# Tokens and hidden rows split into fp16 parts first and turned by transposing DMAs, in a cross-attention block with an MLP

## What is computed

```
q  = LN(x) @ Wq.T + bq ;  k, v = LN(ctx) @ Wk.T + bk, LN(ctx) @ Wv.T + bv
s  = q k.T / sqrt(32) - scale[h] * |xy_q - xy_k| + offset[h] ;  masked keys: -inf
x1 = x + softmax(s) v @ Wo.T + bo
out = x1 + gelu(LN(x1) @ W1.T + b1) @ W2.T + b2        (W1: 2048 x 512)
```

## Time and profile before

| | us |
|---|---|
| median of 3 runs | 1339.89 (1337.30 to 1341.35) |
| profiled execution | 1340.12 |
| its span, first to last instruction | 1338.3 |
| TensorE busy | 1265.7 |
| VectorE, ScalarE, GpSimd busy | 888.0, 831.9, 752.0 |
| share of the sixteen DMA engines, hardware queue | 67.7% |

### The profile page before, as it was taken

How to read it: one execution, slowest core, us unless ns; L and a number is a source line. 1 busy time by engine, 2 the same in 40 slices (tenths; PEclk the granted TensorE clock), 3 DMA queues, 4 the chain that set the end, 5 groups by cost and what they waited for, 6 DMA issues and landing times.

```text
span 1338.3 us, 29112 instructions
## 1 busy us (share of the span) xinstructions
PE 1265.7 (95%) x10624; PEld 881.7 (66%) x10624; DVE 888.0 (66%) x2299; ACT 831.9 (62%) x1905; POOL 752.0 (56%) x871
## 2 busy tenths in 40 slices
PE   5777668999999999999999999999999999999998
PEld 5556336666767676766667676767677676766664
DVE  6577777857667586867677675868676775656311
ACT  4566667766666666666666666666667676664231
POOL 2244556765756576665647565766656575647310
PEclk9775789999999999999999999999999999999999
DMA  6336769676867776775858676777868686657334
GB/s 232 101 76 157 194 166 216 139 186 143 201 150 185 148 179 157 177 173 150 189 146 202 142 174 162 171 173 161 181 146 194 147 188 135 164 144 182 89 109 142
DMA packets 366830, 216.58 MB, mean 162 GB/s; under 512 B 282192, under 2 KB 307040, under 8 KB 366688
## 3 DMA queue, kind: packets, MB, share of 16 engines
q1 hardware_dynamic: 366688, 214.73, 67.7%
HBM read 109.66 MB, written 12.58 MB: 91 GB/s over the span
## 4 chain that ended last, share of the span: by engine, by line
PE 85%; DMA 4%; ACT 4%; DVE 3%; SPq 2%; issue 1%; POOL 0%; DVEq 0%; ACTq 0%
PE ps_down L585 24%; PE ps_up L571 24%; PE ps_qk L500 11%; PE ps_vo L523 6%; PE ps_vo L526 6%; PE ps_s L537 4%; PE ps_pv L552 4%; DMA c_stage<-in_w 3%; PE ps_pv L558 2%; PE ps_pv L479 2%; ACT square_half L648 1%; SPq L333 1%; PE ps_vo L486 1%; SPq L342 1%; PE ps_up L450 1%
## 5 line engine op out<-in xcount | busy, mean ns | idle before, releaser
L984 DVE CUSTOM_DVE_ANT_0 soft<-ps_s,soft,factor 128x256 f32<-128x256 f32 x512 | 226.6, 480 | 266.5 <-PE ps_s L537 265.4
L571 PE MATMUL ps_up<-hT,w 128*128 128x256 f16 x3072 | 378.5, 273 | 0.0
L585 PE MATMUL ps_down<-w,hid 128*128 128x512 f16 x1536 | 372.6, 379 | 0.6 <-DMA w<-x_scratch 0.3
L571 PEld LDWEIGHTS ps_up<-hT,w 128*128 128x128 f16 x3072 | 301.1, 98 | 87.8
L1156 POOL TENSOR_SCALAR p_nat<-soft 128x512 f16<-128x512 f32 x256 | 182.4, 712 | 268.4 <-ACT soft L704 250.7
L704 ACT ACTIVATE soft<-soft,neg_max 128x256 f32<-128x256 f32 x512 | 255.3, 501 | 106.1 <-DVE neg_max L984 100.7
L736 ACT ACTIVATE u<-ps_up,bias,up_scale 128x256 f32<-128x256 f32 x256 | 143.4, 560 | 172.7 <-PE ps_up L571 171.4
L1163 POOL TENSOR_SCALAR soft<-dist,scale_neg,offset 128x512 f32<-128x512 f32 x256 | 237.9, 929 | 3.3 <-DVE p_nat L995 3.3
L585 PEld LDWEIGHTS ps_down<-w,hid 128*128 128x128 f16 x1536 | 148.3, 97 | 133.7 <-DMA w<-x_scratch 2.4
L995 DVE SCALAR_TENSOR_TENSOR p_nat<-soft,p_nat 128x512 f16<-128x512 f32 x256 | 200.2, 782 | 0.5 <-POOL p_nat L1156 0.5
L697 ACT ACTIVATE qk_parts<-ps_qk,bias_qkv 128x512 f16<-128x512 f32 x128 | 87.7, 685 | 86.8 <-DMA stack<-stack 43.4
(11 more groups left out here) (119 smaller groups left out, 1586.7 us busy)
## 6 DMA issues: line engine op xcount, KB each, us to landing
w<-x_scratch SPq DMA_DIRECT2D x256, 256.0 KB, 2.8
stack<-qk_parts SPq DMA_DIRECT2D x256, 96.0 KB
raw<-in_ctx SPq DMA_DIRECT2D x32, 256.0 KB, 3.4
raw<-in_x SPq DMA_DIRECT2D x32, 256.0 KB, 3.3
c_stage<-in_w SPq DMA_DIRECT2D x8, 1024.0 KB, 6.6
x<-in_x SPq DMA_DIRECT2D x32, 256.0 KB, 4.2
out<-x SPq DMA_DIRECT2D x32, 256.0 KB, 3.3
tok_rows<-in_tok_xy SPq DMA_DIRECT2D x16, 256.0 KB, 4.0
```

The costliest lines, as they stand in the source:

```text
L571: mm = e.matmul(ps_up[s % 2][:, 0:L], w_1_sb[:, wp, k, m * P:(m + 1) * P], hT[:, b % 2, xp, k, :], start=(k, wp, xp) == (0, 0, 0), stop=(k ...
L585: mm = e.matmul(ps_down[tt][:], hid[:, chunk % HID_RING, i, hp, tt * P:(tt + 1) * P], w_2_sb[:, s % W2_RING, wp, :], start=(m == 0 and (hp ...
L984: e.tensor_tensor_reduce(soft[:, ring, lc, :], ps_s[:, lc * T:(lc + 1) * T], soft[:, ring, lc, :], factor[:, 0:1], 3.0e38, ALU.add, ALU.mi ...
```

## The change

x_nat and h_nat are new: a normalised tile, still by token, as two fp16 parts side by side, 128 x 1024, one buffer each. ScalarE writes the high part (`x_hi`, `h_hi`) and VectorE the low part (`x_lo`, `h_lo`) from SBUF; SyncE turns both by one transposing DMA (`x_turn`, `h_turn`), of the shape of p_turn's, into xT and hT, whose layout becomes [buffer, which, token tile, part and k, 128]. The fp32 transposes on TensorE are gone, and with them the users of ps_pv and ps_vo beside attention and projections. Slots of batch 0: norm_apply -24 + 4n as before, x_hi and x_lo -23 + 4n, x_turn -22 + 4n; h_apply 26 and 28 (later in VectorE's order within the slot), h_hi and h_lo 27 and 29, h_turn 28 and 30. The parts of a tile wait until the tile before has been turned. To make room, soft has 4 entries for 5 and pT 5 for 6, and bias_tile(i) moves from slot i - 2 to slot i - 1.

```diff
-        SOFT_RING, NAT_RING, PT_RING, STACK_RING, DIST_RING, X1_RING, U_RING, HID_RING, W2_RING = 5, 4, 6, 2, 2, 6, 3, 2, 3
+        SOFT_RING, NAT_RING, PT_RING, STACK_RING, DIST_RING, X1_RING, U_RING, HID_RING, W2_RING = 4, 4, 5, 2, 2, 6, 3, 2, 3
...
-        xT = sb("xT", [P, 2, 2, 2, KT, L], F16)
+        x_nat = sb("x_nat", [P, 2, D], F16)
+        xT = sb("xT", [P, 2, 2, 2, 2 * KT, P], F16)
...
-        hT = sb("hT", [P, 2, 2, KT, L], F16)
+        h_nat = sb("h_nat", [P, 2, D], F16)
+        hT = sb("hT", [P, 2, 2, 2 * KT, P], F16)
...
-        X_TURN, V_PROJ, O_PROJ, H_TURN = -23, (1, 4), (24, 26), (28, 30)
+        X_APPLY, V_PROJ, O_PROJ, H_APPLY = -24, (1, 4), (24, 26), (26, 28)
...
             def load_tile(b, n):
-                gate.wait_ge(s_xtr, n_tile(b - 1, n))
+                gate.wait_ge(s_xlo, n_tile(b - 1, n))
...
+            def x_turn(b, n):
+                gate.wait_ge(s_xlo, n_tile(b, n))
+                gate.wait_ge(s_qk, n_qk(4 * (b - 2) + 3, n // 2))
+                gate.wait_ge(s_v, n_half(b - 2, 1))
+                e.dma_start_transpose(xT[:, b % 2, n // 2, n % 2, :, :], x_nat[:].rearrange("p w d -> p (w d)")).then_inc(s_xt, DMA)
+
+            def h_turn(b, tt):
+                gate.wait_ge(s_hlo, n_half(b, tt))
+                gate.wait_ge(s_m1, MT * (b - 1))
+                e.dma_start_transpose(hT[:, b % 2, tt, :, :], h_nat[:].rearrange("p w d -> p (w d)")).then_inc(s_ht, DMA)
...
                     p_turn(i)
+                for n in range(4):
+                    for b in due(slot, X_APPLY + 2 + 4 * n, BATCH, B):
+                        x_turn(b, n)
+                for tt in range(LC):
+                    for b in due(slot, H_APPLY[tt] + 2, BATCH, B):
+                        h_turn(b, tt)
...
-            def x_turn(b, n):
-                gate.wait_ge(s_ap, n_tile(b, n))
-                gate.wait_ge(s_id, ID_IDENT)
-                gate.wait_ge(s_xlo, n_tile(b, n) - 1)
-                gate.wait_ge(s_y, 4 * (b - 2) + n + 1)
-                for k in range(KT):
-                    tr = e.transpose(ps_pv[:, k * P:(k + 1) * P], raw[:, n, k * P:(k + 1) * P], ident[:])
-                tr.then_inc(s_xtr)
-
-            def h_turn(b, tt):
-                gate.wait_ge(s_hap, n_half(b, tt))
-                gate.wait_ge(*vo_empty(("h", b, tt)))
-                for k in range(KT):
-                    tr = e.transpose(ps_vo[:, k * P:(k + 1) * P], x1_n[:, k * P:(k + 1) * P], ident[:])
-                tr.then_inc(s_htr)
...
-                        gate.wait_ge(s_xlo, n_tile(b, 2 * which + 1))
+                        gate.wait_ge(s_xt, DMA * n_tile(b, 2 * which + 1))
...
-                                              xT[:, b % 2, which, xp, k, :], start=(k, wp, xp) == (0, 0, 0), stop=last)
+                                              xT[:, b % 2, which, :, xp * KT + k, :], start=(k, wp, xp) == (0, 0, 0), stop=last)
...
-                gate.wait_ge(s_xlo, min(G + 8, 4 * B))
...
-                gate.wait_ge(s_hlo, n_half(b, 1))
+                gate.wait_ge(s_ht, DMA * n_half(b, 1))
...
             def x_hi(b, n):
-                gate.wait_ge(s_xtr, n_tile(b, n))
-                gate.wait_ge(s_qk, n_qk(4 * (b - 2) + 3, n // 2))
-                gate.wait_ge(s_v, n_half(b - 2, 1))
-                e.activation(xT_parts(b, n)[HI], turned(ps_pv), ACT.Copy).then_inc(s_xhi)
+                gate.wait_ge(s_ap, n_tile(b, n))
+                gate.wait_ge(s_xt, DMA * (n_tile(b, n) - 1))
+                e.activation(x_nat[:, HI, :], raw[:, n, :], ACT.Copy).then_inc(s_xhi)
 
             def h_hi(b, tt):
-                gate.wait_ge(s_htr, n_half(b, tt))
-                gate.wait_ge(s_m1, MT * (b - 1))
-                e.activation(hT_parts(b, tt)[HI], turned(ps_vo), ACT.Copy).then_inc(s_hhi)
+                gate.wait_ge(s_hap, n_half(b, tt))
+                gate.wait_ge(s_ht, DMA * (n_half(b, tt) - 1))
+                e.activation(h_nat[:, HI, :], x1_n[:], ACT.Copy).then_inc(s_hhi)
...
-                    for b in due(slot, X_TURN + 1 + 4 * n, BATCH, B):
+                    for b in due(slot, X_APPLY + 1 + 4 * n, BATCH, B):
                         x_hi(b, n)
                 for tt in range(LC):
-                    for b in due(slot, H_TURN[tt] + 1, BATCH, B):
+                    for b in due(slot, H_APPLY[tt] + 1, BATCH, B):
                         h_hi(b, tt)
...
-                e.tensor_tensor(lo, turned(ps_pv), hi, ALU.subtract).then_inc(s_xlo)
+                e.tensor_tensor(x_nat[:, LO, :], raw[:, n, :], x_nat[:, HI, :], ALU.subtract).then_inc(s_xlo)
...
-                e.tensor_tensor(lo, turned(ps_vo), hi, ALU.subtract).then_inc(s_hlo)
+                e.tensor_tensor(h_nat[:, LO, :], x1_n[:], h_nat[:, HI, :], ALU.subtract).then_inc(s_hlo)
...
-                gate.wait_ge(s_htr, t)
+                gate.wait_ge(s_hlo, t)
...
-                    for b in due(slot, X_TURN - 1 + 4 * n, BATCH, B):
+                    for b in due(slot, X_APPLY + 4 * n, BATCH, B):
                         norm_apply(b, n)
...
-                    for b in due(slot, H_TURN[tt] - 1, BATCH, B):
-                        h_apply(b, tt)
...
-                    for b in due(slot, X_TURN + 2 + 4 * n, BATCH, B):
+                    for b in due(slot, X_APPLY + 1 + 4 * n, BATCH, B):
                         x_lo(b, n)
...
-                    for b in due(slot, H_TURN[tt] + 1, BATCH, B):
+                    for b in due(slot, H_APPLY[tt], BATCH, B):
+                        h_apply(b, tt)
+                    for b in due(slot, H_APPLY[tt] + 1, BATCH, B):
                         h_lo(b, tt)
...
-                for i in due(slot, -2, ITEM, N_ITEMS):
+                for i in due(slot, -1, ITEM, N_ITEMS):
                     bias_tile(i)
```

More of the change, by code:

```diff
@@ L184, in build_block @@
         s_raw, s_st, s_ag, s_ve, s_rs, s_ap = sems("s_raw", 4), sem("s_st"), sem("s_ag"), sem("s_ve"), sem("s_rs"), sem("s_ap")
-        s_xtr, s_xhi, s_xlo = sem("s_xtr"), sem("s_xhi"), sem("s_xlo")
+        s_xhi, s_xlo, s_xt = sem("s_xhi"), sem("s_xlo"), sem("s_xt")
         s_qk, s_qkhi, s_qklo, s_stack = sem("s_qk"), sem("s_qkhi"), sem("s_qklo"), sems("s_stack", STACK_RING)
@@ L193, in build_block @@
         s_hst, s_hag, s_hve, s_hrs, s_hap = [sem(n) for n in ("s_hst", "s_hag", "s_hve", "s_hrs", "s_hap")]
-        s_htr, s_hhi, s_hlo = sem("s_htr"), sem("s_hhi"), sem("s_hlo")
+        s_hhi, s_hlo, s_ht = sem("s_hhi"), sem("s_hlo"), sem("s_ht")
         s_m1, s_u, s_gelu, s_hidhi, s_hidlo, s_m2, s_out = [
@@ L248, in build_block @@
             for tt in range(2):
-                vo_uses += [("h", b, tt) for b in due(slot, H_TURN[tt], BATCH, B)]
                 vo_uses += [("v", b, tt) for b in due(slot, V_PROJ[tt], BATCH, B)]
@@ L256, in vo_empty @@
             if use not in vo_before:
-                return s_xlo, 0
+                return s_vlo, 0
             kind, b, n = vo_before[use]
-            return {"v": (s_vlo, n_half(b, n)), "o": (s_x1, n_half(b, n)), "h": (s_hlo, n_half(b, n))}[kind]
+            return {"v": (s_vlo, n_half(b, n)), "o": (s_x1, n_half(b, n))}[kind]
         x_rows = x.rearrange("b (c p) d -> (b c) p d", p=P)
@@ L277, in pair @@
             return slice(2 * which, 2 * which + 2)
-        def xT_parts(b, n):
-            tok = (n % 2) * P
-            return [xT[:, b % 2, n // 2, part, :, tok:tok + P] for part in (HI, LO)]
-        def hT_parts(b, tt):
-            return [hT[:, b % 2, part, :, tt * P:(tt + 1) * P] for part in (HI, LO)]
-        def turned(ps):
-            return ps[:].rearrange("p (k t) -> p k t", k=KT)
         def qk_of(which):
@@ L509, in vo_project @@
                     kind, b, tt = use
-                    if kind == "h":
-                        continue
                     if kind == "v":
-                        gate.wait_ge(s_xlo, n_tile(b, tt))
+                        gate.wait_ge(s_xt, DMA * n_tile(b, tt))
                         gate.wait_ge(s_wlo, AT[SEC_V] + 1)
@@ L522, in vo_project @@
                             if kind == "v":
-                                mm = e.matmul(ps_vo[:], xT[:, b % 2, 0, xp, k, tt * P:(tt + 1) * P],
+                                mm = e.matmul(ps_vo[:], xT[:, b % 2, 0, tt, xp * KT + k, :],
                                               w_sec[SEC_V][:, wp, k, :], start=first, stop=last)
@@ L555, in attend @@
                 gate.wait_ge(s_inv, G + 1)
+                gate.wait_ge(s_id, ID_IDENT)
                 for lc in range(LC):
@@ L570, in mlp_up @@
                     for wp, xp in PASSES:
-                        mm = e.matmul(ps_up[s % 2][:, 0:L], w_1_sb[:, wp, k, m * P:(m + 1) * P], hT[:, b % 2, xp, k, :],
+                        mm = e.matmul(ps_up[s % 2][:, 0:L], w_1_sb[:, wp, k, m * P:(m + 1) * P], hT[:, b % 2, :, xp * KT + k, :],
                                       start=(k, wp, xp) == (0, 0, 0), stop=(k, wp, xp) == (KT - 1,) + PASSES[-1])
@@ L615, in tensor_program @@
```

(14 more changed lines are left out.)

## The result

| | before | after |
|---|---|---|
| median | 1340.62 us | 1386.01 us (1383.95 to 1387.81) |
| span of the profiled execution | 1338.3 us | 1385.5 us |
| mean granted clock of TensorE | 0.962 | 0.939 |
| 400 to 550 us: TensorE busy, DMA share | 150.00 us, 0.73 | 142.07 us, 0.85 |

The account below looks back on a forecast made before the run. TensorE, busy 95% of the span and full from about 250 us, was taken as the bound. 1340.1 - 33.9 (transposes) + 33.6 (stall) + 5 (start-up) = 1345 us; range 1306 to 1362.

Parts of the forecast that it names:

- What is taken away: On TensorE from 250 us to the end, 77 tiles of transposes at 0.44 us each go: 33.9 us off the path.
- The new wait: h_hi(b, 1) on ScalarE waits for h_turn(b, 0), delaying TensorE's scores(31): 2.4 us in each of 14 batches, 33.6 us.
- the landing: Time from h_turn's issue on SyncE until its transposed tile has landed: taken as 3.1 us.
- A: End of the attend of slot 28 on TensorE, the zero of the predicted chain; h_hi was to start at A + 4.5.
- the section on VectorE: x_lo and h_lo read SBUF, 0.78 us against 0.68 before; 96 x 0.1 us more, taken as hidden.
- The rings: pT's shorter ring moves SyncE's work by about 1.3 us; the soft ring with later bias_tile on GpSimd costs nothing.
- Start-up: Six c_stage loads delayed 1.3 us each, h_turn(0, 0) 1.3, less 2 to 6 for transposes: +5 us, between -2 and +10.
- The ring's term: In the start-up a second p_turn stands ahead of each of six c_stage loads: 6 x 1.3 = 7.8 us.
- Rival 2: Stack copies on SyncE land later and delay the query projection: 1357 to 1383 us, chance 0.20.
- Rival 1: The stall ahead of TensorE's scores is hidden: 1308 us, to 1325 if half hidden; chance 0.22.
- Rival 3: The transposing DMA is much slower than taken; at the longest landing, 8.0 us, the time is 1413 us; chance 0.02.
- What would show it: TensorE busy 50 to 60 us less, 2 to 3 us gap before scores per batch, ScalarE waiting some 3 us before h_hi.

Follow-up runs that it names:

- 1328.7: x_lo and h_lo issued one slot later, right behind score_max, against the changed kernel with pT's ring back at 6: 1328.7 us (0.9912 to before).

## Why the prediction was wrong, by its steps

- **What is taken away, 33.9 us: right.** The intervals between attends that hold no gap fell from 20.00, 19.56 and 18.26 to 19.12, 19.12 and 17.83 us, and the ledger closes within 1.2 us for four kernels. The two-run layout of xT and hT costs nothing that shows.
- **The new wait: mechanism, place and order right, price too low.** 14 gaps of 2.1 to 4.5 us, 44.3 us in all, where I had 14 x 2.4 = 33.6. The mis-sized terms are the landing (3.1 to 5.0 us after the issue where I took 3.1, so h_hi starts at A + 4.6 to A + 6.5, A + 5.1 in the mean, and not 4.5) and x_lo, 1.10 us where I put 0.68 in the chain and 0.78 in the section on VectorE.
- **The missing term: the clock.** A sum of TensorE's work and its gaps leaves out what a gap does to the work behind it: 20.5 us by the ledger, 19.7 by TensorE's busy time, the largest single error. Nothing in the trace of before had a gap there to show it; I should have asked what the granted clock does after a gap, which the start-up shows (0.73 from 60 to 200 us, with TensorE busy 47 of 60 and 54 of 80 us).
- **The rings: direction right, one term costed at nothing was not nothing.** "GpSimd has 37% free and I cost it at nothing" used a share of the span for a question of order. The bias tile stood behind an instruction that waits. Shorter soft ring and later bias tile by themselves cost 18 us, and 11 of these come back when the tile stands ahead of h_rstd. What they cost inside the changed kernel was not tried by itself.
- **Start-up: +14.1 and not +5.** The ring's term came out right here, 7.5 us return with its entry for my 7.8, but partly by luck: on the kernel before the same entry costs 16. But the 2 to 6 us that I took back for removed transposes did not come; the first attend is 5.4 us later instead, and the chain there shows x_turn(0, 1) issued behind the weights' loads and landing after 8.55 us. That those loads are the cause was not confirmed: with them moved the first attend gained 1.4.
- **Rival 2, the stack copies:** did not happen; those intervals are the ones that got shorter. ScalarE's wait for the copies did grow, from 43.4 to 160.5 us over the run, but the query projection had room. **Rival 1:** its 1308 needs all gaps gone; 1328.7 is how far I came. **Rival 3:** h_turn's landings are 3.0 us at least, 3.2 in the median, 5.0 at most. An estimate from the Trainium skill's 1309 ns a block (VectorE: DVE Perf Modes, The three transpose paths), for eight blocks one after the other, is 10.5; the trace goes on disagreeing for this shape.
- **What would show it:** the wait of ScalarE, the gap at the scores released by VectorE and the later p_turn are all in the profile. "Busy time down by 50 to 60 us" was wrong twice: all 96 tiles at 0.44 are 42 us, which is what the kernel with pT's ring at 6 shows (1223.4 us busy for 1265.7), and matmuls at the lower clock count as busy for longer, so only 18 were left. The DMA engines' share, 0.84 to 0.87 between 400 and 1150 us, was my 0.86.

The range failed too: its upper end, 1362, came from another rival, and the forecast's own bounds, 1335 to 1356, held no term for the clock and a start-up of at most +10. With the measured gaps, 44.3 in place of 33.6, and +14.1 the sum would have been 1364.6; 20.5 for the clock and one gap of 2.2 us elsewhere make it the 1387.3 us of the profiled execution.

## What to carry to other kernels

When a transfer shares an in-order queue with one whose wait is moved, price the buffer that the transfer frees, not the transfer: one ring entry was worth 45 us here because h_turn stood behind a p_turn. An engine with a third of its time free still delays what stands behind a waiting instruction on it, so read the order, not the share. And when TensorE is full, a gap can cost more than itself: here gaps of 2.7 us and more mostly cost another 1.6 to 2.9 us, gaps of 1.83 us about 0.2.
